# Value and x blocks mixed in four pieces, two PSUM bank pairs in the last half slot, and a reordered start and end of an attention-plus-FP8 kernel

## Chip, cores and metric

One core of one Trainium2 chip. The metric is the device time of one execution in microseconds (us), as the median of several runs of the same kernel.

## What is computed

Sixteen sequences of 512 tokens and 256 channels, all float32. Each goes through a pre-norm attention layer with 16 heads of 16 channels, and then a pre-norm linear layer whose input is rounded to FP8:

```python
x = x + attn(layernorm(x), qkv_w, qkv_b, proj_w, proj_b)
# attn: qkv = x @ qkv_w.T + qkv_b; softmax(q k^T / 4) v; out @ proj_w.T + proj_b
x = x + ffn(layernorm(x), weight_fp8, bias, input_scale, weight_scale)
# ffn: clip to +-448, round to float8_e4m3, times w_dq, + bias
```

## The kernel before

The five engines run hand-written programs that meet at semaphores. The unit is a **slot** of 32 **steps**. Slot u works on several sequences at once: it projects sequence u (queries, keys, values), takes row maxima of the scores of sequence u-1, computes transposed scores, exponentials and weighted values of sequences u-2 (steps 0 to 15) and u-1 (steps 16 to 31), and finishes output projection, second norm and linear layer of sequences u-2 and u-3. There is a slot 0 that only prepares, slots 1 to 16, and slot 17 (`LAST_SLOT`), which has only 16 steps of transposed scores, for sequence 15. A tail (`finish` on each engine) ends the last sequence.

Within a step TensorE (PE) issues, in a fixed order, `scores_t` of half g=0 (L551, into `ps_t[:, 0]`), `scores` g=1 (L570, into `ps_s`), `scores_t` g=1, `scores` g=0, then whatever extra block the tables at the top name for that step, and on odd steps `values` (L591). Other engines follow the same order of steps: ScalarE (ACT) does two exponentials (`exps`, L709) per step and copies blocks out of PSUM; VectorE (DVE) takes maxima (`maxima`, L874), sums for the norms (`ln1_sum`, L881), negates and splits the maxima (`split_max`, L921 and L923) and rounds; GpSimd (POOL) normalizes x into `xn` (`layernorm_x`, L1122 and L1133), splits numbers into high and low parts and does the FP8 rounding; SyncE (SP) issues transfers.

The waits that matter here: a `scores_t` waits until the exponential of one step earlier has read its half of `ps_t`; a `scores` waits for the maximum of two steps earlier; at every eighth step the maxima are transposed into `ps_s[:, 1, 0]` (`transpose_max`, L483), and the `scores` of the next odd step wait until VectorE has split them. All extra blocks share the one bank `ps_m`, and `take_bank` makes a block wait for the reader of the block ahead of it. In a usual slot the value projection (`project_v`, L475, 12 matmuls each) stands at steps 20 and 22, the transposes of the next x (`transpose_x`, L412, four each) at steps 24 and 26, the transposes of the rounded values (`transpose_hq`, L514) at step 14, copied in one piece by `copy_hqT` (L757), and `linear` (L531) at steps 16 and 18.

In slot 1 the x of sequence 1 is transposed at steps 0 and 2, and the norm sums of sequence 2 (`ln1_sum`) begin at step 7, on data that `load(2, 0)` brings; SP issues that load behind all stacking transfers of sequence 0 (`first_slot`, `stack`, L309).

Of the kernel before, what the change touches and what calls it, by code (L numbers as in the profile page):

```python
# [42 lines left out]
LAST_ROUND = 8  # L43
LAST_SLOT = NSLOT - 2
FILL_STEPS = range(3, 12)
# [20 lines left out]
LN1_SUM = (7, 12, 13, 15)  # L66
LN1_END = 17
# [4 lines left out]
WARM_FIRST = 3  # L72


def block_kernel(nc, x, qkv_wT, qk_bT, v_bT, proj_wT, proj_b, lin_wT, lin_b, in_scale, w_scale, eye, out):
# [4 lines left out]
    with ExitStack() as ctx:  # L80
# [27 lines left out]
        mv1 = sb("mv1", [P, NJ, 2])  # L108
        nm1 = sb("nm1", [P, NJ])
# [22 lines left out]
        mv2 = sb("mv2", [P, NJ, 2])  # L132
        nm2 = sb("nm2", [P, NJ])
# [34 lines left out]
        half_set = sem("half_set")  # L168
        bias_done = sem("bias_done")
# [52 lines left out]
        res_ready = sem("res_ready")  # L222
        rs2_pow = sem("rs2_pow")
# [19 lines left out]
        def bias_column(b, n):  # L243

            column = 2 * NT + n if b == 0 and n < 2 else (n % 2) * NT + n // 2
            return b_qk[:, column:column + 1]

# [19 lines left out]
        def _(sp):  # L267
# [58 lines left out]
            def first_slot():  # L326

                sp.wait_ge(ones, 1)
# [14 lines left out]
                for n in (2, 3):  # L343
                    stack(0, 0, n)
                load(2, 0)

            def slot(u, par, present):
# [5 lines left out]
                if present(-2):  # L353
                    load(u + 2, par)
                if present(0):
                    stack(u, par, 0)
                if present(1):
                    rows(u - 1, 1 - par, 0)
# [27 lines left out]
        def _(pe):  # L386
            bank_user = [None, 0, 0]

            def take_bank(name, n, b):

                last, m, before = bank_user
                if last in ("transpose_x", "project_qk", "project_v"):
                    reader, value = {"transpose_x": (xnT_ready, 2 * before), "project_qk": (whole_ready, 4 * before),
                                     "project_v": (v_ready, 2 * before)}[last]
                    pe.wait_ge(reader, value + m + 1)
                elif last == "project_out":
                    pe.wait_ge(h_ready, 2 * before + m + 1)
                elif last == "transpose_hq":
                    pe.wait_ge(hqT_ready, before + 1)
                elif last == "linear":  # L400
                    pe.wait_ge(y_ready, 2 * before + m + 1)
                bank_user[:] = [name, n, b]

            def transpose_x(u, c):

                first = u == 0
                bank = ps_t[:, c, :] if first else ps_m[:]
                if not first:
                    take_bank("transpose_x", c, u)
                pe.wait_ge(xn_ready, u + 1)  # L410
                for j in range(NJ):
                    last = nc.tensor.transpose(bank[:, j * P:(j + 1) * P], xn[:, j, c * P:(c + 1) * P], ident[:])  # L412
                last.then_inc(xt_done, 1)
# [17 lines left out]
            def project_first(n):  # L431
# [5 lines left out]
                for m, (pw, px) in enumerate(FIRST_PAIRS):  # L437
                    for c in range(NC):
                        if n == 0:
                            if m == 0:  # L440
                                pe.wait_ge(wqkv_ready, 4)
                                pe.wait_ge(xnT_ready, c + 1)
# [9 lines left out]
            def first_slot():  # L452
# [65 lines left out]
            def linear(b, half, bank=None):  # L518
# [17 lines left out]
            def scores_t(b, par, s, g):  # L536
# [4 lines left out]
                if s % QUARTER == 0 and g == 0:  # L541
# [3 lines left out]
                    if b == 0 and s == 0:  # L545
                        pe.wait_ge(v_ready, 2)
# [788 lines left out]
```

## Time and profile before

| | |
|---|---|
| median of 3 runs | 969.11 us (968.7 to 970.22) |
| the profiled execution's own time | 968.59 us |
| its span in the trace | 966.8 us |
| busy share of the span | PE 96%, DVE 87%, ACT 68%, POOL 53% |
| mean granted TensorE clock | 0.974 of full |

The profile's busy time of a matmul is modelled, so 96% on PE does not mean that no matmul waits: the waits show as start times that lie further apart than the work between them needs. A timeline row gives start, duration, engine, line, operation, and in brackets the idle time before it and what ended it.

### The profile page before, as it was taken

How to read it: one execution, taken by the hardware profiler on the slowest of the kernel's cores; microseconds unless marked ns; L12 is line 12 of the kernel's file. 1: busy time of each engine (PE TensorE's matmuls, PEld its weight loads, DVE VectorE, ACT ScalarE, POOL GpSimd, SP SyncE). 2: the span in 40 equal slices, each digit the busy share in tenths (PEclk: the TensorE clock that was granted, in tenths of full speed). 3: DMA queues.
4: the chain of work that ended last, by engine and by line, in shares of the span. 5: the costliest groups of instructions: out<-in, count | busy, mean ns of one | idle time of the engine just before them, and what ended most of it. 6: DMA issues, size and time to landing. Idle time of an engine off the chain costs nothing.

```text
span 966.8 us, 16811 instructions
## 1 busy us (share of the span) xinstructions
PE 930.0 (96%) x5847; PEld 439.4 (45%) x5847; DVE 843.8 (87%) x1264; ACT 656.4 (68%) x1209; POOL 515.9 (53%) x528
## 2 busy tenths in 40 slices
PE   7799999999999999999999999999999999999993
PEld 4343444444444454544444444444444454433342
DVE  5678889898999989898998989899898989989846
ACT  3157777777777777767677776767777776776760
POOL 4522428467373847647383754738285573715222
PEclk9769999999999999999999999999999999999996
DMA  6971635438083554717265472817556280731010
GB/s 174 159 91 44 107 52 99 79 62 138 29 142 53 100 78 77 124 40 140 44 115 64 83 116 50 140 34 128 72 74 105 35 136 10 136 42 35 13 45 23
DMA packets 46350, 79.45 MB, mean 82 GB/s; under 512 B 10104, under 2 KB 13304, under 8 KB 46264
## 3 DMA queue, kind: packets, MB, share of 16 engines
q1 hardware_dynamic: 45976, 77.97, 47.1%
q8 instruction: 47, 0.77, 0.4%
q10 hardware_dynamic: 288, 0.39, 0.3%
q14 instruction: 39, 0.32, 0.2%
HBM read 18.42 MB, written 8.39 MB: 28 GB/s over the span
## 4 chain that ended last, share of the span: by engine, by line
PE 92%; DVE 2%; ACT 2%; SPq 1%; DMA 1%; issue 1%; ACTq 0%; POOL 0%; DVEq 0%; POOLq 0%
PE ps_t L551 29%; PE ps_o L591 26%; PE ps_m L426 10%; PE ps_s L570 8%; PE ps_m L475 5%; PE ps_m L499 5%; PE ps_m L531 3%; PE ps_m L412 1%; ACT pt L709 1%; PE ps_s L483 1%; DMA xin<-in_x 1%; SPq L309 1%; PE ps_m L514 1%; DVE mx L874 0%; PE ps_s L692 0%
## 5 line engine op out<-in xcount | busy, mean ns | idle before, releaser
L709 ACT ACTIVATE pt<-ps_t 128x512 f32<-128x512 f32 x1024 | 558.0, 598 | 213.9 <-PE ps_t L551 210.5
L874 DVE TENSOR_REDUCE mx<-ps_s 128x2 f32<-128x1024 f32 x512 | 615.3, 1209 | 57.4 <-PE ps_s L570 53.7
L551 PE MATMUL ps_t<-qs,ks 50*128 50x512 f32 x1024 | 391.9, 455 | 8.2 <-ACT pt L709 7.9
L570 PE MATMUL ps_s<-ks,qs 48*128 48x512 f32 x1024 | 380.7, 463 | 8.0 <-DVE nmax L923 4.1
L551 PEld LDWEIGHTS ps_t<-qs,ks 50*128 50x128 f32 x1024 | 164.0, 185 | 296.3 <-ACT pt L709 214.0
L591 PE MATMUL ps_o<-pt,vt 128*32 128x512 f32 x2048 | 272.6, 605 | 0.0
L1176 POOL TENSOR_TENSOR on<-ot,rden 128x256 f32<-128x256 f32 x63 | 39.3, 624 | 243.2 <-DVE rden L935 243.2
L570 PEld LDWEIGHTS ps_s<-ks,qs 48*128 48x128 f32 x1024 | 158.4, 188 | 18.9 <-issue 11.8
L426 PE MATMUL ps_m<-xnT_p,wqkv_p 128*128 128x512 f32 x360 | 109.9, 428 | 1.0 <-POOL xnT_p L1145 1.0
L1167 POOL TENSOR_TENSOR parts<-parts 128x512 f32<-128x512 f32 x60 | 81.3, 1356 | 4.9
L591 PEld LDWEIGHTS ps_o<-pt,vt 128*32 128x32 f32 x2048 | 40.4, 108 | 86.1 <-issue 85.1
L426 PEld LDWEIGHTS ps_m<-xnT_p,wqkv_p 128*128 128x128 f32 x360 | 62.3, 193 | 36.2 <-issue 27.0
L1151 POOL TENSOR_TENSOR oT_p<-oT,oT_p 128x512 fp32r<-128x512 f32 x31 | 39.9, 1287 | 57.2 <-ACT oT_p L735 57.2
L751 ACT ACTIVATE parts<-ps_m,b_qk 128x512 f32<-128x512 f32 x60 | 41.3, 688 | 32.6 <-PE ps_m L426 28.1
L931 DVE STREAM_TRANSPOSE ot<-ps_o 128x512 f32<-128x512 f32 x64 | 45.2, 706 | 11.6 <-PE ps_o L591 11.6
L499 PE MATMUL ps_m<-wproj_p,oT_p 128*128 128x256 f32 x360 | 54.5, 294 | 0.0
L475 PE MATMUL ps_m<-wqkv_p,xnT_p 128*128 128x256 f32 x360 | 51.1, 292 | 0.0
L499 PEld LDWEIGHTS ps_m<-wproj_p,oT_p 128*128 128x128 f32 x360 | 45.7, 189 | 11.0 <-issue 11.0
L475 PEld LDWEIGHTS ps_m<-wqkv_p,xnT_p 128*128 128x128 f32 x360 | 45.0, 192 | 11.1 <-issue 11.1
L1165 POOL CAST parts<-parts 128x512 fp32r<-128x512 f32 x60 | 36.8, 614 | 16.1 <-ACT parts L751 16.1
L1207 POOL TENSOR_TENSOR hn<-hn,xres 128x1024 f32<-128x1024 f32 x14 | 33.3, 2380 | 12.7 <-DVE xres L963 12.7
L1145 POOL TENSOR_TENSOR xnT_p<-xn,xnT_p 128x512 fp32r<-128x512 f32 x30 | 38.4, 1280 | 2.4
(113 smaller groups left out, 763.3 us busy)
## 6 DMA issues: line engine op xcount, KB each, us to landing
qs<-parts SPq DMA_DIRECT2D x186, 128.0 KB, 4.6
ks<-parts SPq DMA_DIRECT2D x186, 128.0 KB, 5.4
xin<-in_x SPq DMA_DIRECT2D x16, 512.0 KB, 3.6
xres<-in_x SPq DMA_DIRECT2D x16, 512.0 KB, 5.8
out<-h SPq DMA_DIRECT2D x31, 256.0 KB, 2.1
qs<-nmax SPq DMA_DIRECT2D x256, 4.0 KB
pt<-in_qkv_wT SPq DMA_DIRECT2D x1, 768.0 KB, 5.2
qs<-parts SPq DMA_DIRECT2D x12, 64.0 KB, 3.6
```

The lines of the kernel that those rows point to most:

```text
L426: last = nc.tensor.matmul(bank, wqkv_p[:, pw, c, first:first + P], xnT_p[:, px, c, :], start=m == 0, stop=m == 5)
L475: last = nc.tensor.matmul(bank[:, j * D:(j + 1) * D], xnT_p[:, px, c, tok], wqkv_p[:, pw, c, 2 * D:3 * D], start=(m == 0 and c == 0), stop ...
L499: last = nc.tensor.matmul(bank[:, j * D:(j + 1) * D], oT_p[:, px, t, tok], wproj_p[:, pw, t, :], start=(m == 0 and t == 0), stop=(m == 2 a ...
L551: nc.tensor.matmul(ps_t[:, g, :], ks[par][rows, slot, keys], qs[par][rows, slot, :], start=True, stop=True).then_inc(st_done, 1)
L570: done = nc.tensor.matmul(ps_s[:, s % 2, g, :], qs[par][rows, slot, queries], ks[par][rows, slot, :], start=True, stop=True)
L591: last = nc.tensor.matmul(ps_o[32 * i:32 * i + VW, :], vt[par][:, 2 * kp + a, head, :], pt[n % 2][:, i, a, :], start=(kp == 0 and a == 0), ...
L709: nc.scalar.activation(pt[n % 2][:, w % 2 + 2 * a, w // 2, :], ps_t[:, a, :], ACT.Exp, scale=SCALE).then_inc(exp_done, 1)
L751: nc.scalar.activation(parts[:, n, 1, :], bank, ACT.Identity, bias=bias).then_inc(whole_ready, 1)
L874: dve.tensor_reduce(mx[:, r, :, s % QUARTER], ps_s[:, s % 2, :, :], AX_X, ALU.max).then_inc(max_done, 1)
L931: dve.transpose(ot[:].rearrange("p a c -> p (a c)"), ps_o[:]).then_inc(ot_ready, 1)
L1151: pool.tensor_tensor(oT_p[:, 1, t, :], oT[:], oT_p[:, 0, t, :].bitcast(F32), ALU.subtract).then_inc(oT_low, 1)
L1167: pool.tensor_tensor(parts[:, n, 1, :], parts[:, n, 1, :], parts[:, n, 0, :], ALU.subtract).then_inc(low_ready, 1)
```

## The change

- **Blocks mixed.** `project_v` and `transpose_x` become `values_and_x`: at each of the steps 20, 22, 24 and 26, six value matmuls into the first half of `ps_m` and two transposes into the second half. ScalarE copies 128x256 four times for v and four times for x. The norm sums of x move from steps 7, 12, 13, 15 (end 17) to 5, 7, 10, 12 (end 13), and GpSimd's `layernorm_x` moves ahead of `low_oT`.
- **Rounded values in two halves.** `copy_hqT` copies one half at step 14 and one at step 15.
- **Norm constants.** The mean is subtracted directly and the added epsilon lies in a third column, so that one reduction replaces two small VectorE operations per norm.
- **Last half slot.** `scores_t` of odd steps goes to `ps_s[:, 0]`, so each half waits for an exponential two steps back; fill matmuls stand at steps 2, 4, 6, 8 only; the rounding (`round_last`) moves from step 8 to 4, the end of the norm from 3 to 2, and GpSimd's `layernorm_h` to the front.
- **Tail.** Both `values` come before `project_last`; ScalarE normalizes the last two token columns of `hn`; 10 and 30 unread fill matmuls are issued while TensorE would wait.
- **Start.** The x of sequence 1 is transposed in slot 0, behind 5 unread matmuls; one unread matmul follows each of 13 of the steps 0 to 15 of slot 1; `load(2, 0)` is SP's first transfer of its slot 0; VectorE does the norm of sequence 2 before slot 1; half of the key stacking goes to ScalarE's queue; the query-key projections of slot 1 move to steps 4, 6, 14 and 16/18.

```diff
-LAST_ROUND = 8
+LAST_ROUND = 4
+LAST_END = 2
...
+FILL_VALUES = 10
+FILL_NORM = 30
-FILL_STEPS = range(3, 12)
+FILL_STEPS = (2, 4, 6, 8)
...
-PROJECT_QK_1 = ((4,), (6,), (8,), (10, 12))
+PROJECT_QK_1 = ((4,), (6,), (14,), (16, 18))
-PROJECT_V = (20, 22)
-TRANSPOSE_X = (24, 26)
-TRANSPOSE_X1 = (0, 2)
+VALUES_AND_X = (20, 22, 24, 26)
-LN1_SUM = (7, 12, 13, 15)
-LN1_END = 17
+LN1_SUM = (5, 7, 10, 12)
+LN1_END = 13
+WARM_SCORES = 5
+WARM_STEPS = (0, 1, 2, 3, 5, 7, 8, 9, 10, 11, 12, 13, 15)
...
+        def t_bank(b, s, g):
+
+            if b == B - 1 and s > HALF_STEPS and s % 2:
+                return ps_s[:, 0, g, :]
+            return ps_t[:, g, :]
...
             def first_slot():
 
+                load(2, 0)
                 sp.wait_ge(ones, 1)
...
-                for n in (2, 3):
-                    stack(0, 0, n)
-                load(2, 0)
+                stack(0, 0, 2)
...
+            def values_and_x(u, i):
+
+                take_bank("values_and_x", i, u)
+                project_values(ps_m[:, 0:D], u, i)
+                if u < B - 1:
+                    c, half = i // 2, i % 2
+                    pe.wait_ge(xn_ready, u + 2)
+                    for j in range(2):
+                        last = nc.tensor.transpose(ps_m[:, D + j * P:D + (j + 1) * P],
+                                                   xn[:, 2 * half + j, c * P:(c + 1) * P], ident[:])
+                    last.then_inc(xt_done, 1)
...
+                elif b == B - 1 and s > HALF_STEPS:
+                    pe.wait_ge(exp_done, 2 * STEPS * b + 2 * s + g - 3)
...
+                    if u == 1 and s in WARM_STEPS:
+                        unread(WARM_STEP)
...
+            def unread(count):
+
+                for i in range(count):
+                    nc.tensor.matmul(ps_t[:, 1, :], wqkv_p[:, 0, 0, 0:P], wqkv_p[:, 0, 0, 0:S], start=True, stop=True)
...
             def finish(b):
                 values(b, b % 2, UNITS - 1, 0)
+                values(b, b % 2, UNITS - 1, 1)
                 pe.wait_ge(oT_high, NT * b + 1)
-                pe.wait_ge(nmax_split, 8 * b + 8)
                 project_last(0, PAIRS[0:3:2], False)
-                values(b, b % 2, UNITS - 1, 1)
                 pe.wait_ge(oT_low, NT * b + 1)
                 project_last(0, PAIRS[1:2], False)
+                unread(FILL_VALUES)
...
                 project_last(1, PAIRS[1:2], True)
+                unread(FILL_NORM)
...
-            def copy_hqT(b):
-                act.wait_ge(xq_done, b + 1)
-                if past(b):
-                    act.wait_ge(lin_done, 2 * b)
-                nc.scalar.copy(hqT[:].rearrange("p c n -> p (c n)"), ps_m[:].bitcast(BF16)).then_inc(hqT_ready, 1)
+            def copy_hqT(b, half):
+
+                if half == 0:
+                    act.wait_ge(xq_done, b + 1)
+                    if past(b):
+                        act.wait_ge(lin_done, 2 * b)
+                tok = slice(2 * half * P, 2 * (half + 1) * P)
+                nc.scalar.copy(hqT[:, :, tok],
+                               ps_m[:].bitcast(BF16).rearrange("p (c n) -> p c n", c=NC)[:, :, tok]).then_inc(hqT_ready, 1)
...
+                for j in range(2, NJ):
+                    act.wait_ge(centred, j - 1)
+                    act.wait_ge(hn_ready, b + j - 1)
+                    nc.scalar.activation(hn[:, j, :], hn[:, j, :], ACT.Copy, scale=rs2[:, j:j + 1]).then_inc(hn_ready, 1)
...
-                dve.tensor_scalar(nm1[:], mv1[:, :, 0], -1.0, None, ALU.mult).then_inc(ln1_ready, 1)
-                dve.tensor_scalar(ve1[:], mv1[:, :, 1], EPS, None, ALU.add).then_inc(ln1_ready, 1)
+                dve.tensor_reduce(ve1[:], mv1[:, :, 1:3], AX_X, ALU.add).then_inc(ln1_ready, 1)
...
             def last_slot(b):
 
-                pool.wait_ge(h_ready, 2 * (b - 1) + 2)
+                layernorm_h(b - 1)
+                out_divide(b, 1)
+                pool.wait_ge(hq_ready, b)
                 pool.tensor_tensor(xin[0][:], h[:], b_lin[:].unsqueeze(1).to_broadcast([P, NJ, D]),
                                    ALU.add).then_inc(hb_ready, 1)
-                out_divide(b, 1)
-                layernorm_h(b - 1)
...
                 if present(0) and u > 0:
                     split(u, 3)
+                if present(-1) and u != 1:
+                    layernorm_x(u + 1, 1 - par)
                 if present(2):
                     low_oT(u - 2, 0)
-                if present(-1):
-                    layernorm_x(u + 1, 1 - par)
```

How the rows move on the engines at three places. First ScalarE in a usual slot, from step 14 on: `pt` are the exponentials, `hqT` the rounded values, `vt` and `xn` the copies of the value and x blocks, `oT_p` a copy of the attention output. Before:

```order
L757 CAST hqT<-ps_m 128x1024
L709 ACTIVATE pt<-ps_t 128x512 x12
L718 COPY vt<-ps_m 128x32x16
L709 ACTIVATE pt<-ps_t 128x512 x4
L718 COPY vt<-ps_m 128x32x16
L709 ACTIVATE pt<-ps_t 128x512 x2
L735 CAST oT_p<-oT 128x512
L709 ACTIVATE pt<-ps_t 128x512 x2
L728 COPY xn<-ps_m 128x4x128
L709 ACTIVATE pt<-ps_t 128x512 x4
```

With the change:

```order
L822 CAST hqT<-ps_m 128x2x256
L759 ACTIVATE pt<-ps_t 128x512 x2
L822 CAST hqT<-ps_m 128x2x256
L759 ACTIVATE pt<-ps_t 128x512 x10
L767 COPY vt<-ps_m 128x16x16
L780 COPY xn<-ps_m 128x2x128
L759 ACTIVATE pt<-ps_t 128x512 x4
L767 COPY vt<-ps_m 128x16x16
L780 COPY xn<-ps_m 128x2x128
L759 ACTIVATE pt<-ps_t 128x512 x2
```

The one copy of 128x1024 has become two, with the two exponentials of step 15 between them, and each step of 20 to 26 now ends with one small copy of v and one of x.

TensorE in the last half slot, steps 2 to 5: `ps_t<-qs,ks` are transposed scores, `ps_s<-wqkv_p` unread fill matmuls, `ps_o` the weighted values. Before:

```order
L551 MATMUL ps_t<-qs,ks 128x512 x4
L637 MATMUL ps_s<-wqkv_p 128x512
L591 MATMUL ps_o<-pt,vt 32x512 x4
L551 MATMUL ps_t<-qs,ks 128x512 x2
L637 MATMUL ps_s<-wqkv_p 128x512 x2
L551 MATMUL ps_t<-qs,ks 128x512 x2
L637 MATMUL ps_s<-wqkv_p 128x512
L591 MATMUL ps_o<-pt,vt 32x512 x4
```

With the change (where `ps_s<-qs,ks` are transposed scores too, in the second bank pair):

```order
L597 MATMUL ps_s<-qs,ks 128x512 x2
L637 MATMUL ps_o<-pt,vt 32x512 x4
L597 MATMUL ps_t<-qs,ks 128x512 x2
L681 MATMUL ps_s<-wqkv_p 128x512
L597 MATMUL ps_s<-qs,ks 128x512 x2
L637 MATMUL ps_o<-pt,vt 32x512 x4
L597 MATMUL ps_t<-qs,ks 128x512 x2
L681 MATMUL ps_s<-wqkv_p 128x512
```

The transposed scores alternate between two bank pairs, and the fill of the odd steps is gone.

TensorE at the end of slot 0 and in the first steps of slot 1: `ps_t<-wqkv_p,xnT_p` is the value projection of sequence 0, `<-ident,xn` are transposes of x of sequence 1, `ps_s<-ks,qs` are scores. Before:

```order
L475 MATMUL ps_t<-wqkv_p,xnT_p 128x256 x24
L570 MATMUL ps_s<-ks,qs 128x512 x2
L412 MATMUL ps_m<-ident,xn 128x128 x4
L570 MATMUL ps_s<-ks,qs 128x512 x4
L412 MATMUL ps_m<-ident,xn 128x128 x4
L570 MATMUL ps_s<-ks,qs 128x512 x4
L426 MATMUL ps_m<-xnT_p,wqkv_p 128x512 x6
```

With the change:

```order
L505 MATMUL ps_t<-wqkv_p,xnT_p 128x256 x24
L496 MATMUL ps_s<-wqkv_p 128x512 x5
L440 MATMUL ps_o<-ident,xn 128x128 x4
L440 MATMUL ps_t<-ident,xn 128x128 x4
L616 MATMUL ps_s<-ks,qs 128x512 x2
L703 MATMUL ps_t<-wqkv_p 128x512
L616 MATMUL ps_s<-ks,qs 128x512 x2
```

All eight transposes stand ahead of the first scores, behind five unread matmuls, and an unread matmul follows the scores.

## Rows read from the trace of the kernel before

**Rows 1.** The page's chain of waits (part 4): shares of the span by engine.

```profile
PE 92%; DVE 2%; ACT 2%; SPq 1%; DMA 1%; issue 1%; ACTq 0%; POOL 0%; DVEq 0%; POOLq 0%
```

**Rows 2.** Windows: stretch, its us, busy us of five engines, granted clock, DMA share, GB/s.

```profile
22.80:33.00 10.20, 8.93 (x29) 5.02 (x27) 6.63 (x7) 1.86 (x3) 6.99 (x9) 0.50 0.82 127
...
43.30:63.70 20.40, 19.15 (x59) 10.42 (x63) 15.89 (x23) 7.36 (x13) 5.07 (x7) 0.50 0.76 100
...
947.80:966.80 19.00, 6.77 (x30) 5.20 (x29) 13.23 (x36) 1.33 (x3) 4.97 (x6) 0.50 0.08 29
```

**Rows 3.** Timeline of slot 7, steps 20 to 28 (VectorE's row from its own timeline).

```profile
393.73 0.49 PE L551 MATMUL ps_t<-qs,ks 50*128 50x512 f32 x1
...
394.39 1.63 PE L475 MATMUL ps_m<-wqkv_p,xnT_p 128*128 128x256 f32 x12
...
400.57 1.07 PE L591 MATMUL ps_o<-pt,vt 128*32 128x512 f32 x8
...
402.35 0.60 PE L412 MATMUL ps_m<-ident,xn 128*128 128x128 f32 x4
...
402.86 0.28 DVE L923 SCALAR_TENSOR_TENSOR nmax<-ps_s,nmax 16x128 f32<-16x128 f32 x1
...
403.29 0.51 PE L570 MATMUL ps_s<-ks,qs 48*128 48x512 f32 x2
...
408.02 0.50 PE L551 MATMUL ps_t<-qs,ks 50*128 50x512 f32 x1
```

**Rows 4.** Timeline of slot 7, steps 14 to 16.

```profile
383.45 0.50 PE L551 MATMUL ps_t<-qs,ks 50*128 50x512 f32 x1
...
384.67 0.49 PE L551 MATMUL ps_t<-qs,ks 50*128 50x512 f32 x1
...
384.96 1.02 ACT L757 CAST hqT<-ps_m 128x1024 fp32r<-128x1024 bf16 x1
...
386.62 0.47 PE L551 MATMUL ps_t<-qs,ks 50*128 50x512 f32 x1
...
386.83 0.42 DVE L881 BATCH_NORM_STATS2 st<-xin 128x6 f32<-128x256 f32 x1
```

**Rows 5.** Groups of instructions by form: ScalarE's exponentials and copies out of PSUM.

```profile
L709 ACT ACTIVATE pt<-ps_t 128x512 f32<-128x512 f32 x1024 | 558.0, 598 | 213.9 <-PE ps_t L551 210.5
...
L728 ACT COPY xn<-ps_m 128x512 f32<-128x512 f32 x30 | 17.8, 592 | 4.5 <-PE ps_m L412 4.5
...
L812 ACT CAST hqT<-ps_m 128x256 fp32r<-128x256 bf16 x1 | 0.4, 372 | 1.5 <-PE ps_m L684 1.5
```

**Rows 6.** Timeline of slot 7 on GpSimd: the normalized x of sequence 8.

```profile
393.27 2.18 POOL L1133 TENSOR_SCALAR xn<-xin,nm,rs 128x256 f32<-128x256 f32 x4 [0.34 <-POOL rs L1122]
```

**Rows 7.** Timeline of slot 1 (VectorE and PE), and the start of slot 2.

```profile
35.06 1.23 DVE L874 TENSOR_REDUCE mx<-ps_s 128x2 f32<-128x1024 f32 x1 [0.15 <-PE ps_s L570]
...
41.02 0.43 DVE L881 BATCH_NORM_STATS2 st<-xin 128x6 f32<-128x256 f32 x1 [4.74 <-DMA xin<-in_x]
...
41.87 3.46 DVE L874 TENSOR_REDUCE mx<-ps_s 128x2 f32<-128x1024 f32 x3
...
59.57 2.93 PE L475 MATMUL ps_m<-wqkv_p,xnT_p 128*128 128x256 f32 x12
...
81.21 0.50 PE L551 MATMUL ps_t<-qs,ks 50*128 50x512 f32 x1
```

**Rows 8.** Timeline of the last half slot (slot 17, from step 0) to its last values.

```profile
913.10 0.50 PE L551 MATMUL ps_t<-qs,ks 50*128 50x512 f32 x2
...
928.85 1.23 DVE L980 TENSOR_TENSOR hq<-hn,xres 128x1024 bf16<-128x1024 f32 x1
...
942.76 1.06 PE L591 MATMUL ps_o<-pt,vt 128*32 128x512 f32 x8
```

**Rows 9.** The chain of waits in order of time, in the tail: start, us, what.

```profile
948.58 0.70 DVE h L1070
...
958.00 2.08 PE ps_s L692 x8
```

More of the change, by code:

```diff
@@ L398, in take_bank @@
                 elif last == "transpose_hq":
-                    pe.wait_ge(hqT_ready, before + 1)
+                    pe.wait_ge(hqT_ready, 2 * before + 2)
                 elif last == "linear":
                     pe.wait_ge(y_ready, 2 * before + m + 1)
+                elif last == "bias":
+                    pe.wait_ge(const_v, 3)
                 bank_user[:] = [name, n, b]
             def transpose_x(u, c):
-                first = u == 0
-                bank = ps_t[:, c, :] if first else ps_m[:]
-                if not first:
+                bank = x_bank(u, c)
+                if u > 1:
                     take_bank("transpose_x", c, u)
+                if u == 1 and c == 1:
+                    pe.wait_ge(v_ready, 2)
                 pe.wait_ge(xn_ready, u + 1)
@@ new lines, in copy_first_v, with copy_x_half @@
+            def copy_first_v(half):
+                act.wait_ge(v_done, 2 * half + 2)
+                act.wait_ge(ones, 3)
+                nc.scalar.copy(vt[0][:, 2 * half:2 * half + 2, :, 0:HD],
+                               ps_t[:, half, :].rearrange("p (j h e) -> p j h e", j=2, h=H)).then_inc(v_ready, 2)
+            def copy_x_half(b, i):
+                c, half = i // 2, i % 2
+                act.wait_ge(xt_done, 4 * b + i + 1)
+                nc.scalar.copy(xn[:, 2 * half:2 * half + 2, c * P:(c + 1) * P],
+                               ps_m[:, D:2 * D].rearrange("p (j m) -> p j m", j=2)).then_inc(xnT_ready, 1)
@@ L776, in first_slot @@
                 copy_qk(0, 0, 3)
-                copy_v(0, 0, 0)
-                copy_v(0, 0, 1)
+                copy_first_v(0)
+                copy_first_v(1)
+                for c in range(NC):
+                    copy_xnT(1, c)
+                act.wait_ge(low_ready, 4)
+                for r, part in enumerate(K_PARTS):
+                    for g in range(2):
+                        rows = slice(HALF * g + HD * r, HALF * g + HD * (r + 1))
+                        act.dma_start(ks[0][rows, NS:2 * NS, :].bitcast(F32),
+                                      parts[HALF * g:HALF * (g + 1), 3, part, :]).then_inc(stacked[1][0], 16)
             def slot(u, par, present):
@@ L862, in prepare @@
                                              op0=ALU.add, op1=ALU.subtract).then_inc(low_ready, 1)
-            def finish_bias():
-                dve.wait_ge(bias_done, 1)
-                dve.tensor_tensor(b_proj[:], ps_o[:, 0:D], b_proj[:], ALU.add).then_inc(const_v, 1)
+                finish_bias()
+                for j in range(NJ):
+                    ln1_sum(2, 0, j)
+                ln1_finish(2)
             def maxima(b, s):
```

214 lines of the change are left out of this document (119 added, 95 removed).

## The prediction

> **What bounds the kernel now.** I read the chain of waits first. TensorE (PE) holds 92% of it [rows 1], so time can only go where TensorE waits or where its clock is low; ScalarE and GpSimd matter through what they make it wait for. The windows by clock came next: TensorE is granted half of its clock, its lower level of 1.2 GHz, in the stretches 22.8 to 33.0, 43.3 to 63.7 and from 947.8 to the end [rows 2], that is in slot 1 and in the tail. In between it is at the full level. Last I read timelines of one usual slot, of slot 1, of the last half slot and of the tail. The reader is to compare start times there: the busy figure of PE hides waits, since the ends of matmuls are modelled.
>
> In a usual slot one step's four score matmuls take 0.66 us (393.73 to 394.39), and a block of 12 value matmuls 1.63, about 1.56 of which pass before the next start [rows 3]. The `values` of an odd step add about 1.0 (1.07 at 400.57, less overlap). From these, steps 20 to 27 need four pairs of 2 x 0.66 + 1.0 = 2.32, or 9.3 us, two value blocks, 3.1, and two transpose blocks of 0.6 [rows 3], 1.2: 13.6 us. They take 408.02 - 393.73 = 14.3. So 0.7 us is waiting. The larger part can be seen: step 24's transposes start at 402.35 and take 0.60, but the scores of step 25 start at 403.29, because VectorE's second split operation ends only at 402.86 + 0.28 = 403.14 [rows 3]. The rest follows step 26, whose even step is too short for the two exponentials of the loop. The value blocks of steps 20 and 22 hide such latencies; the transposes are too short to.
>
> Steps 14 and 15 show the other wait. Step 14 takes 384.67 - 383.45 = 1.22, step 15 takes 386.62 - 384.67 = 1.95 [rows 4], where 0.66 + 1.0 would do. ScalarE's copy of 1.02 at 384.96 [rows 4] stands ahead of step 15's exponentials, which the transposed scores of step 16 wait for: 0.29 lost.
>
> **The change part by part**, against the profiled execution's 968.59 us (span 966.8 and 1.8 around it; the median of the runs shown, 969.11, is 0.05% above).
>
> *Mixed blocks.* The same matmuls now come in four equal pieces of about (3.1 + 1.2) / 4 = 1.07 us, one in each even step from 20 to 26. The split of the maxima at step 24 then lies beside a piece that runs longer than it does, and every even step is longer than its exponentials need. The 0.7 us go in 14 slots (2 to 15): **-9.8**. Bounds: 0, if other waits fill the gap, and 10. What is added: ScalarE makes eight copies in place of four. A 128x512 copy takes 0.592, a 128x256 copy 0.372 [rows 5], so eight cost 2.98 against 2.37, 0.6 more per slot. It lies beside TensorE: a pair of steps would need 4 exponentials at 0.60 and two copies of 0.37, about 3.1 [rows 5], against TensorE's 2.32 + 1.07 = 3.4. The next wait in line is for x: the first transposes now stand at step 20, about 0.9 us after 394.39, at 395.3, while before, xn is ready at 393.27 + 2.18 = 395.45 [rows 6]. But the sums end four steps earlier, and GpSimd's `layernorm_x` no longer stands behind `low_oT`; I expect xn some 2 us sooner, about 1.5 us early. SP and its loads are not reordered in usual slots. Splitting xnT waits for all four value pieces now, to step 26; its reader is step 2 of the next slot, some 8 us after it is done.
>
> The small norm operations: one reduction for two VectorE operations per norm, beside other work: 0. The two sums of 0.42 [rows 4] that move to steps 5 and 10 load VectorE there by 0.7, where it has gaps; I take 0. If that cover is gone, the maximum of step 14 is late for the scores of step 16, by up to 0.35 per slot, 5 us.
>
> A rule that speaks against the small copies is in the Trainium skill, "VectorE: DVE Perf Modes", section "The TRN2 errata": its table gives every ScalarE instruction a fixed part besides the one that grows with the elements, and it advises tiles of 512 elements or more. The trace agrees: half the elements take 0.372 of 0.592, not a half [rows 5]. A rival below prices that extra as if nothing hid it.
>
> *Copy in two halves.* Two copies at about 0.59 (the size of [rows 5]'s first row) in place of 1.02. Step 15's exponentials start some 0.4 earlier, and `linear` at step 16 still finds the second half about when it arrives. Step 15 falls from 1.95 to about 1.66 in 14 slots (3 to 16): **-4.1**, bounds 0 and -4.1.
>
> *Start.* VectorE's maximum of step 7 ends at 35.06 + 1.23 = 36.29; its next one starts at 41.87, since the norm sum at step 7 stands 4.74 us for a load issued late [rows 7]. About 0.9 of those 5.6 belongs to the split; 4.7 goes, since load and sums now lie in slot 0. The second half-clock stretch lasts 20.4 us with TensorE busy 19.15, VectorE 15.89 [rows 2]; a value block takes 2.93 there [rows 7] against 1.63. At the full level VectorE's 15.9 would bound it: 4.5. In the first half-clock stretch VectorE has 6.63 of 10.2 [rows 2]; up to 3.5 could go, but the first scores come 1.2 later, behind unread matmuls and transposes: 2. Together -11.2 if the clock holds; if it stays low, -3, because 13 unread matmuls at about 0.45 (2.93 / 12 for 256 columns, doubled) then lengthen the steps. I take **-10**, near the first, since TensorE's idle time ahead of the first scores goes, and let part of the first stretch stay low. Half of the key transfers on ScalarE's queue hold it for some 4 us, in which it has nothing to copy.
>
> On the clock, rows show that a TensorE busy 19.15 of 20.4 us was granted 0.50 all through [rows 2]. The Trainium skill, "TensorE: Matmul & The Clock Gate", section "What's actually happening", says the gate opens with recent activity; by that rule alone the unread matmuls would hold the full level, and the sum would be 934.5. The trace agrees only in part: by the row, filling does not do it at once.
>
> *Last half slot.* Step 0 starts at 913.10, the last values end at 942.76 + 1.06 = 943.82 [rows 8]: 30.7 us, in which each transposed score waits for the exponential one step back. With two bank pairs it waits for one two steps back, and TensorE's own work decides: 16 pairs of transposed scores, which run side by side, at 0.43 (the row of 0.50 at 913.10, less overlap), 6.9; ten `values`, 10.0; output projection (12 matmuls), 1.6; hq transposes 0.6; two linear blocks of 8, 2.2; four fills at 0.4, 1.6: 22.9, and 1.1 for the linear block that waits for its copies: 24.0. ScalarE needs 32 x 0.60 [rows 5] and 1.8 of copies, 21. **-6.7**, with both `values` ahead of `project_last` contained in it. The rounding ended at 928.85 + 1.23 = 930.1 [rows 8]; four steps earlier it ends near 926, when TensorE reaches step 10. If it is 3 us late, -3.7 is left.
>
> *Tail.* From 943.8 to 966.8 the chain alternates between VectorE and TensorE at half clock. The first linear block takes 2.08 at 958.00 [rows 9]; at full clock 1.1. Two smaller ones save 0.4 each, and ScalarE takes two normalizations of about 0.3 off VectorE: **-2.3**. Bounds: -3.5, and +5 if the clock falls all the same: 30 unread matmuls at 0.45 are 13.5 us against 8 between the last projection (the row at 948.58) and the hq transposes just ahead of 958.00 [rows 9].
>
> **Sum:** -9.8 - 4.1 - 10 - 6.7 - 2.3 = -32.9: 968.6 - 32.9 = 935.7, or **936 us**.
>
> **The rivals.**
> - *The clock stays low in slot 1, or falls in the tail.* For it: the busy stretch at 0.50 [rows 2]. Start -3 instead of -10, or the tail +5 instead of -2.3: 943 us each.
> - *The steady gain does not come, because other waits, VectorE's sums at steps 5 and 10 first, fill the gaps.* For it: the sums of 0.42 each [rows 4] meet VectorE's other work there; against it: the 3.1 against 3.4 per pair. Without both steady terms: 936 + 13.9 = 950 (0.10).
> - *ScalarE's extra time is all on the path.* The halves cost it 0.6 per slot for v and x and 2 x 0.59 - 1.02 = 0.16 for the rounded values, 14 x 0.76 = 10.6 on top of the rival before: 961 (0.02). This is what the rule of the Trainium skill on the fixed part, "VectorE: DVE Perf Modes", would do where ScalarE ends the waits.
> - *Slower: x is late at step 20.* The transposes stand in TensorE's queue ahead of all scores, so a late xn stops everything. It decides from a POOL chain that ends over 1.5 us later than I expect; slower than before needs 33 / 14 = 2.4 us of standing in each slot, so xn near 397.7 in the time of [rows 6], 2.2 us later than it is today. With 2.6 us: 936 + 36 = 972. Against it: it now has one operation of 1.3 less ahead of it.
> - *The change does not do what it says:* the waits merely move and the clock is unchanged, 968.
>
> **How the numbers follow.** The forecast, 928 to 940: 0.62. Clock rival, 940 to 948: 0.20. Steady gain missing, 948 to 962, with ScalarE's case: 0.12. Slower: 0.02; no change: 0.02; faster still, under 928: 0.02. The range 928 to 948 leaves out the last four, 0.18, and spans the bounds of the start and of the tail. A measurement of this kernel tells some 0.2% from no change. Faster 0.96, same 0.02, slower 0.02.
>
> **What would show it.** Right: in a usual slot steps 20 to 27 take 13.6 and step 15 about 1.7; no idle time of VectorE on an x load in slot 1, slot 2 starting near 71; the granted clock at 1.00 from 33 to beyond 955; the last half slot about 24 us from its step 0 to the last values. Wrong: PE rows of the mixed pieces waiting for POOL's xn or for ScalarE's v and x copies; half-clock windows in slot 1; the hq transposes at step 10 of the last slot waiting for VectorE; the 30 unread matmuls still running when hq is ready.

## The result, and the profile after

The changed kernel takes 1001.12 us (median of 4 runs, 997.08 to 1005.18) against 969.08 (968.70 to 970.22) for the kernel before: 1.033 times as long, with a 95% interval of 1.029 to 1.037. The prediction was 936, and faster. The profiled execution has a span of 995.2 us and a time of 997.08, the fastest of the four. One execution of e1_add_column, its profiled one, took 1582.21 us where five others took 948 to 956; it is left out of every number below.

Three stretches of the two traces stand side by side by the start of slot 2 and of slot 16 (first score matmul of each). To slot 2: 80.1 us, before 81.2. From there to slot 16: 817.3, before 779.5. From slot 16 to the end: 97.8, before 106.1. The end gave nearly what was expected (8.3 of 9.0 us), the start nearly nothing, and the 14 usual slots lost 38 us where 14 were to be won.

The groups of instructions by form show which engine changed, here GpSimd's eight normalizing operations per slot:

```profile
L1219 POOL TENSOR_SCALAR xn<-xin,mv,rs 128x256 f32<-128x256 f32 x60 | 72.6, 1221 | 5.1 <-POOL rs L1208 5.1
L1277 POOL TENSOR_SCALAR hn<-h,mv,rs 128x256 f32<-128x256 f32 x56 | 67.7, 1222 | 3.2 <-POOL rs L1271 3.2
```

Before, four of them took 2.18 us [rows 6], 0.56 each in the same view; now one takes 1.22. The edit had replaced the column `nm` and an addition by the column `mv[:, j, 0:1]` and a subtraction. Four operations are 2.65 us longer, twice per slot. The view of waits says who stood for that (us in total, times, longest):

```profile
PE ps_m L555 <- POOL hq L1297: 17.9, 13, 1.4
PE ps_m L517 <- POOL xn L1219: 13.0, 12, 2.0
```

Neither stands in the same view of before. In the timelines of slot 8, first GpSimd's, then TensorE's, both waits stand in place:

```profile
439.70 4.84 POOL L1277 TENSOR_SCALAR hn<-h,mv,rs 128x256 f32<-128x256 f32 x4 [0.49 <-POOL rs L1271]
...
452.88 2.36 POOL L1297 TENSOR_TENSOR hq<-hn,xres 128x1024 bf16<-128x1024 f32 x1
...
463.32 4.84 POOL L1219 TENSOR_SCALAR xn<-xin,mv,rs 128x256 f32<-128x256 f32 x4 [0.34 <-POOL rs L1208]
```

```profile
455.38 0.61 PE L555 MATMUL ps_m<-ident_b,hq 128*128 128x128 bf16 x8 [1.40 <-POOL hq L1297]
...
465.23 0.98 PE L505 MATMUL ps_m<-wqkv_p,xnT_p 128*128 128x256 f32 x6
468.22 0.44 PE L517 MATMUL ps_m<-ident,xn 128*128 128x128 f32 x2 [2.01 <-POOL xn L1219]
...
469.26 1.76 PE L637 MATMUL ps_o<-pt,vt 128*32 128x512 f32 x8
```

The transposes of hq (step 14) wait 1.40 for hq, those of x (step 20) 2.01 for xn, and the values after them take 1.76 instead of 1.06: the granted clock has fallen. The windows (stretch, its us, busy us of PE, PEld, DVE, ACT, POOL, granted clock, DMA share, GB/s) show that and the start:

```profile
29.20:39.40 10.20, 10.20 (x24) 5.36 (x22) 5.51 (x5) 1.20 (x2) 5.24 (x7) 0.50 1.08 118
...
42.80:53.10 10.30, 10.19 (x24) 4.72 (x23) 7.29 (x7) 0.64 (x1) 4.83 (x4) 0.50 0.70 97
...
80.10:897.40 817.30, 783.27 (x5057) 367.39 (x5053) 712.56 (x1014) 575.00 (x1114) 524.03 (x457) 0.98 0.49 81
...
469.40:473.20 3.80, 3.80 (x18) 1.62 (x14) 2.80 (x3) 2.07 (x4) 2.91 (x3) 0.55 1.08 127
897.40:995.20 97.80, 86.81 (x553) 41.45 (x549) 77.46 (x131) 59.06 (x112) 35.01 (x30) 1.00 0.09 29
```

Between 80 and 897 us the clock was never low before; now it is, for such a stretch, in 9 of the 14 usual slots (the mean clock of each slot is 0.97 or 1.00). The two half-clock stretches of slot 1 are still there, one of them half as long as before [rows 2]. The last half slot and the tail keep the full level, with a first linear block of 1.22 instead of 2.08 [rows 9]. In slot 1 the long operation shows too: xn of sequence 1 takes 4.83, and the first scores stand behind it.

```profile
19.55 4.83 POOL L1219 TENSOR_SCALAR xn<-xin,mv,rs 128x256 f32<-128x256 f32 x4 [0.35 <-POOL rs L1208]
```

```profile
24.43 0.66 PE L440 MATMUL ps_o<-ident,xn 128*128 128x128 f32 x4 [1.46 <-POOL xn L1219]
```

### The profile page after: what moved, and what is told of

Read it like the earlier page. It is cut to its first block, busy times and chain, and to the rows that moved or that the text cites. A ratio compares the mean times of both kernels' runs of the same rounds, so it can differ in the third digit from the quotient of the medians.

```text
span 995.2 us, 17007 instructions
## 1 busy us (share of the span) xinstructions
PE 939.6 (94%) x5896; PEld 445.3 (45%) x5896; DVE 844.6 (85%) x1231; ACT 665.9 (67%) x1287; POOL 596.2 (60%) x528
## 3 DMA queue, kind: packets, MB, share of 16 engines
q10 hardware_dynamic: 768, 1.18, 0.9%
## 4 chain that ended last, share of the span: by engine, by line
PE 38%; POOL 36%; DVE 12%; issue 10%; ACT 1%; SPq 1%; DMA 0%; POOLq 0%; DVEq 0%; ACTq 0%
PE ps_o L637 11%; PE ps_t L597 10%; POOL hn L1277 7%; POOL parts L1253 7%; DVE mx L961 5%; PE ps_s L616 4%; POOL xn L1219 4%; PE ps_m L505 4%; POOL parts L1251 3%; POOL hq L1297 3%; POOL hn L1293 3%; POOL h L1287 3%; DVE st L985 2%; DVE h L1036 2%; PE ps_m L454 2%
## 5 line engine op out<-in xcount | busy, mean ns | idle before, releaser
L759 ACT ACTIVATE pt<-ps_t 128x512 f32<-128x512 f32 x1008 | 548.5, 598 | 204.6 <-PE ps_t L597 202.1
L597 PE MATMUL ps_t<-qs,ks 50*128 50x512 f32 x1008 | 378.2, 453 | 9.2 <-ACT pt L759 7.6
L597 PEld LDWEIGHTS ps_t<-qs,ks 50*128 50x128 f32 x1008 | 161.7, 187 | 291.8 <-ACT pt L759 207.2
L637 PE MATMUL ps_o<-pt,vt 128*32 128x512 f32 x2048 | 278.9, 618 | 0.0
L1219 POOL TENSOR_SCALAR xn<-xin,mv,rs 128x256 f32<-128x256 f32 x60 | 72.6, 1221 | 5.1 <-POOL rs L1208 5.1
L1277 POOL TENSOR_SCALAR hn<-h,mv,rs 128x256 f32<-128x256 f32 x56 | 67.7, 1222 | 3.2 <-POOL rs L1271 3.2
L505 PE MATMUL ps_m<-wqkv_p,xnT_p 128*128 128x256 f32 x360 | 59.6, 302 | 0.0
L1251 POOL CAST parts<-parts 128x512 fp32r<-128x512 f32 x60 | 43.2, 720 | 19.3 <-ACT parts L813 19.3
L505 PEld LDWEIGHTS ps_m<-wqkv_p,xnT_p 128*128 128x128 f32 x360 | 47.7, 194 | 15.5 <-issue 15.5
L1229 POOL CAST xnT_p<-xn 128x512 fp32r<-128x512 f32 x30 | 18.3, 611 | 54.9 <-PE ps_m L505 53.4
```

Of the source, the lines that this page charges most:

```text
L505: last = nc.tensor.matmul(bank, xnT_p[:, px, c, tok], wqkv_p[:, pw, c, 2 * D:3 * D], start=(m == 0 and c == 0), stop=(m == 2 and c == NC - 1))
L597: nc.tensor.matmul(t_bank(b, s, g), ks[par][rows, slot, keys], qs[par][rows, slot, :], start=True, stop=True).then_inc(st_done, 1)
L637: last = nc.tensor.matmul(ps_o[32 * i:32 * i + VW, :], vt[par][:, 2 * kp + a, head, :], pt[n % 2][:, i, a, :], start=(kp == 0 and a == 0), ...
L759: nc.scalar.activation(pt[n % 2][:, w % 2 + 2 * a, w // 2, :], t_bank(b, s, a), ACT.Exp, scale=SCALE).then_inc(exp_done, 1)
L1219: last = pool.tensor_scalar(xn[:, j, :], xin[par][:, j, :], mv1[:, j, 0:1], rs1[:, j:j + 1], ALU.subtract, ALU.mult)
L1251: pool.tensor_copy(parts[:, n, 0, :].bitcast(F32R), parts[:, n, 1, :]).then_inc(high_ready, 1)
```

## The experiments

**Three theories.** 1: a subtraction is dear on GpSimd. 2: a column inside the statistics tile is dear. 3: whatever the operation costs, x is needed too early once its transposes stand at step 20. Four kernels tell them apart.

*e1_add_column.* VectorE negates the means into columns of their own, and GpSimd adds them:

```
+ dve.tensor_scalar(nm1[:], mv1[:, :, 0], -1.0, None, ALU.mult)
- pool.tensor_scalar(xn[:, j, :], xin[par][:, j, :], mv1[:, j, 0:1], rs1[:, j:j + 1], ALU.subtract, ALU.mult)
+ pool.tensor_scalar(xn[:, j, :], xin[par][:, j, :], nm1[:, j:j + 1], rs1[:, j:j + 1], ALU.add, ALU.mult)
```

(and the same for h.) Expected:

> The changed kernel, but VectorE again writes the negated means into contiguous columns of their own, one small operation more per norm, and GpSimd's eight normalizing operations per slot add that column instead of subtracting the mean from where the statistics stand. Theory 1 (GpSimd's subtract with a column is dear) and theory 2 (the column inside the statistics tile is dear) both expect its normalizing operations back at about 559 ns from 1221, steps 14 to 16 and 20 of a usual slot without the waits for hq and xn, a slot at about 54.7 us instead of 58.4, and 997 - 14 x 3.7 - 1.5 (xn of sequence 1) = about 943 us (938 to 950). Theory 3 (x is needed too early at step 20 whatever GpSimd's operation costs, since the mixed pieces put the transposes ahead) expects step 20 still over 2.4 us and more than 969 us.

Measured: 948.1 to 956.3 us in five runs, ratio to before 0.982 (0.980 to 0.984). The rows are taken from the next kernel, whose GpSimd operations are the same.

*e2_add_in_place.* The multiplication by -1 writes the statistics tile itself, and GpSimd adds from `mv[:, j, 0:1]`.

> The changed kernel, but VectorE negates the means in place in the statistics tile (one small operation per norm) and GpSimd adds them from there: the operation is as before the change, the operand's place as after it. Theory 1 (the operation): 559 ns, about 943 us. Theory 2 (the operand's place): 1221 ns, about 997 us.

Measured: 952.0 us (949.7 and 954.4). GpSimd's groups:

```profile
L1221 POOL TENSOR_SCALAR xn<-xin,mv,rs 128x256 f32<-128x256 f32 x60 | 32.4, 554 | 5.1 <-POOL rs L1210 5.1
L1279 POOL TENSOR_SCALAR hn<-h,mv,rs 128x256 f32<-128x256 f32 x56 | 30.2, 554 | 3.2 <-POOL rs L1273 3.2
```

*e3_sub_column.* Means copied into columns of their own, and subtracted.

> The changed kernel, but VectorE copies the means into contiguous columns of their own and GpSimd subtracts them from there: the operand's place is as before the change, the operation as after it. Theory 1 (the operation): 1221 ns, about 997 us. Theory 2 (the operand's place): 559 ns, about 943 us.

Measured: 1003.2 us (997.1 and 1009.4). Its group:

```profile
L1223 POOL TENSOR_SCALAR xn<-xin,nm,rs 128x256 f32<-128x256 f32 x60 | 72.6, 1221 | 5.1 <-POOL rs L1212 5.1
```

*e4_before_sub.* The kernel before, with `nm` holding the mean and the operations subtracting it.

> The kernel before, with one thing changed: the columns hold the mean itself, and the normalizing operations subtract it. Theory 1: GpSimd's operations take 1221 ns, a chain 2.65 us longer twice a slot; xn has some 7 us to spare in this order, hq about 1, so 14 x 1.6 = 23 us slower, about 991 (975 to 1005). Theory 2: 559 ns and 969, as before. Theory 3 (the place of the x transposes is what costs): 1221 ns or not, within 5 us of 969, since nothing waits early for x here.

Measured: 1001.1 us (998.1 to 1002.1), ratio 1.033 (1.032 to 1.035). GpSimd's group and the longest wait in it:

```profile
L1133 POOL TENSOR_SCALAR xn<-xin,nm,rs 128x256 f32<-128x256 f32 x60 | 72.8, 1226 | 5.1 <-POOL rs L1122 5.1
```

```profile
PE ps_m L514 <- POOL hq L1211: 19.3, 13, 1.6
```

What follows: the operation sets the price, not its operand's place (554 with add from the statistics tile, 1221 with subtract from a column). Theory 2 is out. Theory 3 is out as it was put: with the addition step 20 takes 1.77 us (slot 7 of e2). Put alone into the old order, the subtraction costs 32 us: of 29.5 us by the profiles, 28.6 lie between slots 2 and 16, 2.0 per slot at steps 14 to 16, behind the wait for hq; xn has time there. In the new order it costs 49 (1001.1 against 952.0), since x is then late as well.

But e1 and e2 stand at 952, 9 us above what was expected. In e2 a usual slot takes 55.71 us, hardly less than before (55.77): steps 20 to 27 take 13.8 instead of 14.3, but steps 15 and 16 together take 4.38 instead of 3.92. The first transposed scores of steps 15, 16 and 17 of slot 7 in e2, then that of step 17 before (steps 15 and 16 are in [rows 4]):

```profile
380.98 0.50 PE L597 MATMUL ps_t<-qs,ks 50*128 50x512 f32 x1
...
382.86 0.49 PE L597 MATMUL ps_t<-qs,ks 50*128 50x512 f32 x1
...
385.36 0.50 PE L597 MATMUL ps_t<-qs,ks 50*128 50x512 f32 x1
```

```profile
388.59 0.50 PE L551 MATMUL ps_t<-qs,ks 50*128 50x512 f32 x1
```

VectorE's timeline in slot 8 of e2, at steps 3 and 13, and GpSimd's beside step 13:

```profile
419.24 0.17 DVE L995 TENSOR_SCALAR mv<-mv 128x4 f32<-128x4 f32 x1
...
436.81 0.97 DVE L977 TENSOR_SCALAR mv<-mv 128x4 f32<-128x4 f32 x1
437.69 0.15 DVE L978 TENSOR_REDUCE ve<-mv 128x4 f32<-128x8 f32 x1
437.76 2.34 DVE L961 TENSOR_REDUCE mx<-ps_s 128x2 f32<-128x1024 f32 x2
```

```profile
435.35 2.40 POOL L1289 TENSOR_TENSOR h<-h,b_lin 128x1024 f32<-128x1024 f32 x1
```

My own repair cost that: the multiplication of 4 elements a partition takes 0.97 us and ends at 437.78, as GpSimd's addition does (437.75); the maximum of step 14 starts behind it and the scores of step 16 wait for that. The same holds in all 12 slots in which the multiplication starts beside that addition: it takes 0.94 to 0.97 and ends 27 to 34 ns after the addition. The Trainium skill, "SBUF — State Buffer", section "SBUF: two separate sides", says that VectorE and GpSimd share a port pair, that a GpSimd operation, or a VectorE operation in a two-port mode or with two inputs in SBUF, locks it for the whole instruction, and that the other engine then stands. The trace agrees, with those ends.

*e5_negating_reduce.* As e1, but the negated means come from a reduction (the lines below are against e1; h in the same way).

```
- dve.tensor_scalar(nm1[:], mv1[:, :, 0], -1.0, None, ALU.mult)
+ dve.tensor_reduce(nm1[:], mv1[:, :, 0:1], AX_X, ALU.add, negate=True)
```

> As the run that adds a negated column, but the negated means come from a second small reduction on VectorE (which negates its result) instead of a multiplication by -1. In the profile with the mean negated in place, that multiplication takes 0.95 us at step 13 against 0.17 at step 3: it ends as GpSimd's addition of 2.40 us ends, and the maximum of step 14 and the scores of step 16 stand behind it (steps 15 and 16: 2.12 and 2.26). Theory A (VectorE's multiplication waits for GpSimd's running operation, a reduction does not): the reduction takes about 0.15, step 15 about 1.7, step 16 about 1.85, a usual slot 55.71 - 0.8 = 54.9, and 952 - 14 x 0.8 = about 941 us (938 to 945). Theory B (the two sums of 0.42 moved to steps 5 and 10 and the end of the norm at step 13 load VectorE too much in any form): steps 15 and 16 keep at least 4.2 together, 950 us or more.

Measured: 940.6 us (939.9 to 942.5), ratio 0.971 (0.970 to 0.972). Theory A. The reduction is short beside the same GpSimd addition, which runs on for another 0.7 us, in all 12 such slots, and no step waits for hq or xn (VectorE's and GpSimd's timelines in slot 8, then TensorE's in slot 7: first transposed scores of steps 14, 15, 16, 17, 20 and 28):

```profile
428.23 0.16 DVE L979 TENSOR_REDUCE nm<-mv 128x4 f32<-128x4 f32 x1
```

```profile
426.77 2.36 POOL L1291 TENSOR_TENSOR h<-h,b_lin 128x1024 f32<-128x1024 f32 x1
```

```profile
371.95 0.50 PE L599 MATMUL ps_t<-qs,ks 50*128 50x512 f32 x1
...
373.17 0.50 PE L599 MATMUL ps_t<-qs,ks 50*128 50x512 f32 x1
...
375.06 0.50 PE L599 MATMUL ps_t<-qs,ks 50*128 50x512 f32 x1
...
376.87 0.49 PE L599 MATMUL ps_t<-qs,ks 50*128 50x512 f32 x1
...
381.97 0.50 PE L599 MATMUL ps_t<-qs,ks 50*128 50x512 f32 x1
...
395.81 0.50 PE L599 MATMUL ps_t<-qs,ks 50*128 50x512 f32 x1
```

Steps 20 to 27 take 13.84, step 15 takes 1.89, step 16 takes 1.81; a usual slot takes 54.95. This kernel, the change without GpSimd's subtractions, is faster than the kernel before and than the changed one. The remaining runs take single parts of the change out of it.

*e6_hqT_whole.* One copy at step 14, as before: `nc.scalar.copy(hqT[:]..., ps_m[:].bitcast(BF16)).then_inc(hqT_ready, 2)`.

> The kernel with the negating reduction, with ScalarE's copy of the transposed rounded values in one piece at step 14 again (in all slots but the last). If the halves are worth what the prediction took, step 15 goes from about 1.66 to 1.95 and the time rises by 14 x 0.29 = 4.1 us. If the maximum of step 14 ends last at steps 15 and 16 anyway, within 1 us of the run beside it.

Measured: 946.6 us, 6.0 more. In slot 7 of its profile step 15 is back at 1.95 and step 16 at 1.97 (transposed scores start at 375.54, 377.49 and 379.46), and a slot takes 55.17: 14 x 0.22 = 3.1 us. Its profiled execution, 945.1, is its fastest; there 2.7 us lie between slots 2 and 16 and 1.6 ahead of slot 2, where executions differ (below). The rest of the 6.0 no profile shows.

*e7_unmixed.* `VALUES_AND_X = (20, 22, 24, 26)` becomes `PROJECT_V = (20, 22)` and `TRANSPOSE_X = (24, 26)`, with whole blocks and copies as before.

> The kernel with the negating reduction, with the value blocks whole at steps 20 and 22 and the transposes of x whole at steps 24 and 26 again, copied in two pieces each; the sums of the norm stay early. If mixing is worth what the prediction took: 14 x 0.7 = 9.8 us slower than the run beside it; by steps 20 to 27 of the profile with the mean negated in place (13.82, against 14.30 before): 14 x 0.48 = 6.7 us slower. If only other waits move: the same time.

Measured: 949.2 us (948.5 to 951.0), 8.6 more. First transposed scores of steps 20 and 28 in slot 7:

```profile
385.02 0.50 PE L592 MATMUL ps_t<-qs,ks 50*128 50x512 f32 x1
...
399.34 0.50 PE L592 MATMUL ps_t<-qs,ks 50*128 50x512 f32 x1
```

14.32 us, against 13.84. Between slots 2 and 16 its profile is 7.7 us longer than that of e5. So the mixing is worth 7 to 9 us.

*e8_fill_step8.* `if u == 1 and s == 8: unread(2)`, behind the transpose of the maxima.

> The kernel with the negating reduction and two more unread matmuls in slot 1 at step 8, behind the transpose of the maxima, where TensorE stood 0.78 us (34.80 to 35.58) in the profile with the mean negated in place, some 2 us before the granted clock fell to 0.50 for 23.8 us (37.7 to 61.5). If that stand is what lets the clock fall: no half-clock stretch before 50, slot 2 starts at 71 to 74 instead of 78, 4 to 7 us faster than the run beside it. If the clock falls for other reasons: slot 2 still starts at 77 to 79, within 1.5 us of it.

Measured: 940.4 us, no difference (939.0 to 942.9). In its profile the clock falls at 41 instead of 36 and slot 2 starts at 71.9 instead of 73.4. But executions of the same code differ more: slot 2 starts at 73.4, 73.5, 74.6 and 81.7 us in the profiles of e5, e12, e11 and e10, whose code is the same up to there. How the clock goes in slot 1 is not settled by the order alone.

*e9_operations.* Eight forms of the operation, two of them with a single ALU operation, one on each 128x256 tile.

> A measurement, in the kernel with the negating reduction: GpSimd's four normalizing operations per norm get four different pairs of operations on the same 128x256 tile, so x and h aren't normalized here. For x, with two columns: add then multiply, subtract then multiply, multiply then add, multiply then subtract. For h: add a column alone, subtract a column alone, subtract and multiply by constants, add and multiply by constants. If any subtraction is dear on GpSimd, the four with a subtract take about 1221 ns and the others about 555. If only the pair subtract then multiply with two columns is, one takes 1221 and the other seven 555 or less. Its time means nothing.

GpSimd's timeline; the lines of h are a column added, a column subtracted, subtract and multiply by constants, add and multiply by constants; those of x are add then multiply and subtract then multiply, then multiply then add and multiply then subtract:

```profile
425.53 0.94 POOL L1285 TENSOR_SCALAR hn<-h,nmh 128x256 f32<-128x256 f32 x1 [0.49 <-POOL rs L1278]
426.45 0.93 POOL L1287 TENSOR_SCALAR hn<-h,nmh 128x256 f32<-128x256 f32 x1
427.45 1.07 POOL L1289 TENSOR_SCALAR hn<-h 128x256 f32<-128x256 f32 x1
428.49 0.41 POOL L1291 TENSOR_SCALAR hn<-h 128x256 f32<-128x256 f32 x1
...
448.00 1.77 POOL L1227 TENSOR_SCALAR xn<-xin,nm,rs 128x256 f32<-128x256 f32 x2 [0.35 <-POOL rs L1212]
449.76 1.77 POOL L1227 TENSOR_SCALAR xn<-xin,rs,nm 128x256 f32<-128x256 f32 x2
```

Taken singly, on average of 15 sequences, the two of the first row of x are 552 and 1224 ns, those of the second 561 and 1239. Every pair with a subtraction is at 1.07 to 1.24 us and every pair of an addition and a multiplication at 0.41 to 0.56. Neither theory had the single operations: one addition of a column takes 0.94, more than the addition and the multiplication together, and as much as one subtraction. So what is dear is a pair with a subtraction, against the pairs of an addition and a multiplication; why, no run shows.

*e10_no_fill.* `FILL_VALUES = 0`, `FILL_NORM = 0`.

> The kernel with the negating reduction without the 10 and 30 unread matmuls of the tail. If they hold the granted clock: without them it falls in the tail, the first linear block takes about 2.08 again instead of 1.20, the two smaller ones 1.22, 1.5 to 2.5 us slower than the run beside it. If they hold nothing: the same time.

Measured: 942.4 us, 1.7 more; its five runs span 940.3 to 949.4. The first linear block of the tail, here and in e5:

```profile
938.80 2.08 PE L744 MATMUL ps_s<-wlin_p,hqT 128*128 128x256 f32 x8 [0.68 <-ACT hqT L897]
```

```profile
931.48 1.20 PE L744 MATMUL ps_s<-wlin_p,hqT 128*128 128x256 f32 x8 [0.67 <-ACT hqT L897]
```

In all ten other profiles of kernels with the fill this block takes 1.18 to 1.22. From the last values to the end they take 20.8 to 21.7 us, e10 22.3. So the unread matmuls hold the clock there, for this block at least: in e5 it falls at 933.4, right behind it. The 1.7 us fit, though by themselves they lie within what its runs differ.

*e11_one_pair.* `t_bank` returns `ps_t[:, g, :]` always, and the wait is the general one.

> The kernel with the negating reduction, with one bank pair for the transposed scores in the last half slot again (each waits for the exponential one step back); the order of the last values, the rounding and the unread matmuls stay as changed. If the two pairs carry the term of the last half slot: 23.8 us from its step 0 to the last values become 28 to 30.5, 4 to 6.7 us slower than the run beside it. If the other parts carry it: within 1.5 us.

Measured: 944.0 us, 3.4 more. Step 0 of the last half slot and its last values, which end at 921.84:

```profile
894.49 0.50 PE L593 MATMUL ps_t<-qs,ks 50*128 50x512 f32 x2
...
919.06 2.78 PE L633 MATMUL ps_o<-pt,vt 128*32 128x512 f32 x24
```

27.4 us against 23.8 in e5, whose rows are:

```profile
893.74 0.50 PE L599 MATMUL ps_t<-qs,ks 50*128 50x512 f32 x2
...
914.72 2.78 PE L639 MATMUL ps_o<-pt,vt 128*32 128x512 f32 x24
```

The two pairs carry 3.6 of the 6.9 us by which 23.8 lies under the 30.7 of before, a little under what was expected; the other parts carry the rest together, and no run parts them.

*e12_end15.* `LN1_END = 15`.

> The kernel with the negating reduction, with the end of x's norm on VectorE (four aggregations and two reductions, 0.6 us) at step 15 instead of 13, behind the maxima of steps 14 and 15. If the maximum of step 14 (26.07 to 27.29 after the slot's start), for which the scores of step 16 at 27.72 wait, is what keeps steps 15 and 16 at 1.88 and 1.81: both together 3.69 fall to about 3.4, and the time to about 937. If VectorE is late at step 16 in any order, or GpSimd's xn (ready 1.6 us ahead of the transposes at step 20) becomes late: 940 or more.

Measured: 940.3 us, and steps 15 and 16 keep 1.89 and 1.82 although the maximum of step 14 ends 0.4 to 0.5 us sooner. Neither story held: what step 15 waits for is ScalarE. In e5's slot 7 its second transposed score starts at 373.62, as the second exponential of step 14 ends (372.49 + 1.09 = 373.58). TensorE's row, then ScalarE's:

```profile
373.62 0.50 PE L599 MATMUL ps_t<-qs,ks 50*128 50x512 f32 x1
```

```profile
372.49 1.09 ACT L761 ACTIVATE pt<-ps_t 128x512 f32<-128x512 f32 x2 [0.43 <-PE ps_t L599]
373.46 0.59 ACT L824 CAST hqT<-ps_m 128x512 fp32r<-128x512 bf16 x1
```

Step 14 takes 1.22, too little to hide two exponentials behind it. That is read off the trace; no run took it away.

## Why the prediction was wrong

**The step that failed** is in "Mixed blocks": "I expect xn some 2 us sooner, about 1.5 us early", and "The small norm operations: one reduction for two VectorE operations per norm, beside other work: 0". The second counted what left VectorE and nothing of what the edit did on GpSimd, whose eight operations a slot got another operation and another column. The row that would have priced them, 2.18 for four [rows 6], was read as the price of both. The true one was 4.84. The difference between the changed kernel and e5, which differ in that operation and in the reduction that prepares its column, is 995.2 - 939.2 = 56.0 us of profiled span (60.5 by the medians): 49.2 in slots 2 to 15 (3.5 per slot on average: about 1.3 at step 14, 0.6 at steps 15 and 16, 1.1 at step 20, 0.3 in steps 21 and 22), 6.6 ahead of slot 2, 0.2 behind. The 6.6 are no more than executions of e5's code differ there (slot 2 at 73.4 to 81.7), so they can't be put down to the subtraction.

**The rival that came true** is "x is late at step 20", given 0.02. Its mechanism is there, with 13.0 us of standing in 12 waits and 2.0 at most, where it asked for 2.4 a slot; the reason against it ("it now has one operation of 1.3 less ahead of it") left out the 2.65 inside it and the 2.65 of h's chain. More than half of the loss it did not name: 2.0 of the 3.5 us per slot lie at steps 14 to 16, by hq, whose slack no row of the prediction looked at, since nothing there seemed to move.

**The other terms, by e5**, stand in the main. Its profiled span of 939.2 is 27.6 under 966.8, against 32.9 predicted.
- Mixed blocks and the copy in halves, -13.9: -11.3 between slots 2 and 16. The mixing gives 14 x 0.48 by the steps (e7: 8.6 in time) of the -9.8; steps 20 to 27 take 13.84, where 13.6 was worked out. The halves bring step 15 to 1.89, not to 1.66, and step 16 from 1.97 to 1.81: by e6, 0.22 a slot of the 0.29. The 1.66 left out ScalarE: step 14 takes 1.22, and its two exponentials end too late for step 15. With the addition xn was ready at 381.81 in slot 7, 1.6 us ahead of its transposes at 383.43, as the prediction had it:

```profile
379.65 2.16 POOL L1223 TENSOR_SCALAR xn<-xin,nm,rs 128x256 f32<-128x256 f32 x4 [0.34 <-POOL rs L1212]
```

- Start, -10: -7.8 in that profile, and between -9.3 and +0.5 in the others. VectorE's stand for the load is gone where it was looked at (the changed kernel, e2, e5). That e5's profile comes near -10 is luck: half-clock stretches remain in every profile, and "if it stays low, -3" did not bound them (-1.1 in the changed kernel, +0.5 in e10).
- Last half slot, -6.7, and tail, -2.3: -8.5 together. 23.8 us where 24.0 was worked out; the tail 21.7 for 23.0, or 20.8 where the clock held nearly to the end (e11).
- The rule of the Trainium skill on the fixed part of ScalarE's instructions ("VectorE: DVE Perf Modes", section "The TRN2 errata") decided nothing here, as taken: e7 has fewer and larger copies and is slower. The rule of the Trainium skill, "TensorE: Matmul & The Clock Gate", section "What's actually happening", that the gate opens with recent activity, is borne out in the tail (1.20 against 2.08), and not in slot 1, where the changed kernel's TensorE is busy 10.20 of 10.20 us and granted 0.50 (29.2 to 39.4).

## What to carry to other kernels

An edit that "only" swaps an operand or an operation has a price on the engine that runs it: count that instruction again, with a row of the same operation on the same engine, not of the same work. If the engine has a faster form (here the pair of an addition and a multiplication, with the column negated), let another engine prepare it, but not with an operation that waits for the first one. And when a step moves ahead of other work, ask what happens if its input is as late as it is long, for that is how one mis-priced operation is paid twice.

## What was not expected of the hardware

- GpSimd's two-operation instruction on 128x256 fp32 depends on which operations they are: 0.55 us for add and multiply with two columns, 1.22 for subtract and multiply, 0.41 and 1.07 with constants; a lone addition or subtraction of a column takes 0.94 and 0.93. On VectorE the two forms cost the same: the first xn takes 408 ns each before, 410 after.
- A VectorE multiplication on 128x4 took 0.17 us, or 0.97 where a GpSimd operation of 2.4 us was running, ending with it; a reduction at the same place took 0.16.
- In the changed kernel, where TensorE stands up to 1.4 us for hq and 2.0 for xn, the granted clock fell in 9 of 14 usual slots; in e4, with up to 1.6 for hq alone, in 7 of 14; before, in e2 and in e5, without these waits, in none. In e4 a slot (3 to 14) with such a fall takes 58.3 to 58.7 us, one with the wait and no fall 57.3 to 57.9: a wait can cost more than its own length. In the changed kernel the six falls behind hq do not show in the slot's length (58.5 or 58.6 with and without), since step 20 then waits less for xn; the three behind xn do (60.1 to 60.4).
